# Attention outputs of two heads: sixteen 32-column matmuls, or eight of 64 columns with a copy per head

## What is computed

```python
# HEADS = 16, DIM_HEAD = 64, WINDOW = 32; per batch and head, w = 32 queries per window
bk2, bv2 = (look(bk), look(bv))        # the keys and values of the previous and the own window: 64
sim = jnp.einsum('bhwie,bhwje->bhwij', bq, bk2) * QK_SCALE
sim = jnp.where(mask, -jnp.finfo(sim.dtype).max, sim)
attn = jax.nn.softmax(sim, -1)
out = jnp.einsum('bhwij,bhwje->bhwie', attn, bv2)      # <- the product that is changed
```

## Time and profile before

| | us |
|---|---|
| three runs | 2413.82, 2416.41, 2401.31 (median 2413.82) |
| the profiled execution, its time | 2405.99 |
| the profiled execution, its span | 2404.1 |
| TensorE matmul busy | 2066.7 (86%) |
| VectorE busy | 1774.6 (74%) |
| ScalarE busy | 1492.8 (62%) |
| TensorE weight loads busy | 1431.0 (60%) |

### The profile page before, as it was taken

One profiled execution on the slowest core, in us unless ns is written; L12 is line 12 of the kernel. 1 busy time (PEld: TensorE's weight loads), 2 busy tenths in 40 slices (PEclk: granted clock), 3 DMA queues, 4 the chain that ended last, 5 costly groups with the idle time before them and its releaser, 6 DMA issues. The chain is left out here.

```text
span 2404.1 us, 81162 instructions
## 1 busy us (share of the span) xinstructions
PE 2066.7 (86%) x33532; PEld 1431.0 (60%) x33532; DVE 1774.6 (74%) x3984; ACT 1492.8 (62%) x5170; POOL 1256.0 (52%) x869
## 2 busy tenths in 40 slices
PE   5549999899999999989999999999999964763377
PEld 2337767576675766747667576675766732432255
DVE  4669779597795977959779597795977836685754
ACT  2239769497785976849769497684876823451122
POOL 1138668386783857838678386783865701221000
PEclk8679999999999999999999999999999985885699
DMA  2011111111111111111111111111110100001000
GB/s 96 0 36 41 30 31 54 38 44 30 33 53 37 46 28 35 51 37 44 30 35 53 35 44 30 34 51 38 40 30 25 42 1 12 1 0 54 1 0 17
DMA packets 86557, 80.34 MB, mean 33 GB/s; under 512 B 15040, under 2 KB 82624, under 8 KB 85568
## 3 DMA queue, kind: packets, MB, share of 16 engines
q1 hardware_dynamic: 86208, 75.37, 10.9%
HBM read 25.51 MB, written 1.05 MB: 11 GB/s over the span
## 5 line engine op out<-in xcount | busy, mean ns | idle before, releaser
L984 POOL TENSOR_TENSOR RN<-N,minus_half 128x8 f32<-128x8 f32 x384 | 632.6, 1648 | 158.1 <-DVE N L916 157.1
L822 ACT ACTIVATE PB<-PS,NMX 128x64 f32<-128x64 f32 x1536 | 461.9, 312 | 126.2 <-DVE NMX L950 126.0
L663 PE MATMUL PS<-WQ,XS 128*128 128x256 f32 x1536 | 398.7, 383 | 13.9 <-SPq L538 13.0
L822 ACT ACTIVATION_READ_ACCUMULATOR PB<-PS,NMX 128x1 f32 x1536 | 311.1, 203 | 0.0
L979 POOL TENSOR_TENSOR RR<-R1B,R 128x512 f32<-128x512 f32 x192 | 244.4, 1273 | 103.8 <-DVE QK L940 103.8
L979 POOL TENSOR_TENSOR RR<-R 128x512 f32<-128x512 f32 x192 | 245.4, 1278 | 97.7 <-DVE QK L940 97.7
L663 PEld LDWEIGHTS PS<-WQ,XS 128*128 128x128 f32 x1536 | 264.1, 192 | 35.3 <-SPq L538 13.3
L916 DVE TENSOR_REDUCE N<-SQ 128x8 f32<-128x512 f32 x384 | 259.4, 675 | 5.5 <-ACT SQ L810 5.4
L933 DVE TENSOR_TENSOR R<-PS,SINL 128x512 f32<-128x512 f32 x384 | 262.0, 682 | 1.0 <-POOL RR L979 1.0
L940 DVE SCALAR_TENSOR_TENSOR QK<-RN,RR 128x512 f32<-128x512 f32 x384 | 261.2, 680 | 0.0
L650 PE MATMUL PS<-ident,QK 128*128 128x128 f32 x1536 | 252.1, 287 | 1.8 <-DVE QK L940 1.8
(11 more groups left out here) (210 smaller groups left out, 3582.9 us busy)
## 6 DMA issues: line engine op xcount, KB each, us to landing
VS<-XB SPq DMA_DIRECT2D x384, 96.0 KB
VS<-XB SPq DMA_DIRECT2D x288, 32.0 KB
WQ<-in_wqkv SPq DMA_DIRECT2D x40, 192.0 KB, 2.4
WO<-in_wo SPq DMA_DIRECT2D x6, 512.0 KB, 3.7
BIG<-in_wgu SPq DMA_DIRECT2D x1, 2048.0 KB, 8.7
W<-in_w SPq DMA_DIRECT2D x6, 341.0 KB, 4.0
WQ<-in_wqkv SPq DMA_DIRECT2D x1, 1536.0 KB, 12.0
QKS<-in_qks SPq DMA_DIRECT2D x6, 256.0 KB, 3.4
```

The costliest lines, as they stand in the source:

```text
L663: mm = nc.tensor.matmul(PQ[:, (g + 3) % 2, j * 256:(j + 1) * 256], XSb[b][:, t0:t0 + P], WQ[:, pair * 384:pair * 384 + 256], start=True, s ...
L822: ex = nc.scalar.activation(PB[:, g % 2, u, :], SC[:, h, DH * t:DH * t + DH], ACT.Exp, bias=NMX[:, u:u + 1], accum_out=PSUMS[:, g % 2, u:u ...
L984: nc.gpsimd.tensor_tensor(RN[:, g % 2, :], N2[:, g % 2, :], minus_half[:, :], ALU.pow)
```

## The change

L682 becomes eight matmuls. Each has as stationary operand the values of both heads (64 keys x 128 features), and as moving operand the probabilities of both heads for one window (two runs of 32 columns, 128 apart). Its output is 128 partitions x 64 columns, of which two quarters are wanted: head 0's rows with head 0's queries, head 1's rows with head 1's. The other two (one head's values with the other's probabilities) are computed and not read. `PO` is used to column 256 of each bank in place of 128. The copy to `OTS` becomes two copies of 64 partitions, one per head, and the second one gives `o_free`.

```diff
@@ TensorE, attention outputs
                             for w in range(4):
                                 for t in range(2):
-                                    for h in range(2):
-                                        keys = slice(2 * WIN * t, 2 * WIN * t + 2 * WIN)
-                                        vals = VX if w % 2 else VS
-                                        cols = 256 + P * h + WIN * w
-                                        mm = nc.tensor.matmul(
-                                            PO[DH * h:DH * h + DH, t, WIN * w:WIN * w + WIN],
-                                            vals[keys, c, w // 2, DH * h:DH * h + DH],
-                                            XB[keys, g % CH, cols:cols + WIN],
-                                            start=True, stop=True)
+                                    keys = slice(2 * WIN * t, 2 * WIN * t + 2 * WIN)
+                                    vals = VX if w % 2 else VS
+                                    probs_of_heads = XB[keys, g % CH, 256:512].rearrange(
+                                        "p (h w q) -> p w h q", h=2, w=4)[:, w, :, :]
+                                    mm = nc.tensor.matmul(
+                                        PO[:, t, 2 * WIN * w:2 * WIN * w + 2 * WIN]
+                                        .rearrange("p (h q) -> p h q", h=2),
+                                        vals[keys, c, w // 2, :], probs_of_heads,
+                                        start=True, stop=True)
                             mm.then_inc(o_ps.sem, 1)
@@ ScalarE, copy of the attention outputs
-                            nc.scalar.activation(
-                                OTS[:, pair, c * CB * P:(c + 1) * CB * P]
-                                .rearrange("p (j t q) -> p t j q", j=CB, t=2),
-                                PO[:, :, 0:P].rearrange("p t (j q) -> p t j q", j=CB), ACT.Copy)\
-                                .then_inc(o_free.sem, 1)
+                            for h in range(2):
+                                rows = slice(DH * h, DH * h + DH)
+                                o = nc.scalar.activation(
+                                    OTS[rows, pair, c * CB * P:(c + 1) * CB * P]
+                                    .rearrange("p (j t v q) -> p t j v q", j=CB, t=2, v=2),
+                                    PO[rows, :, 0:256].rearrange("p t (j v n q) -> p t j v n q",
+                                                                 j=CB, v=2, n=2)[:, :, :, :, h, :], ACT.Copy)
+                            o.then_inc(o_free.sem, 1)
```

## The result

| | before | after |
|---|---|---|
| runs, median | 2412.14 us (2401.31 to 2416.41, 4 runs) | 2520.63 us (2518.75 to 2521.61, 4 runs) |
| ratio, 95% interval | | 1.0466 (1.0441 to 1.0490) |
| profiled execution, span | 2404.1 us | 2519.5 us |

2520 us was forecast, in a range of 2480 to 2556. The change costs 108 us by the medians and 112 by the ratio.

A forecast was written before the change was run, and what follows sets the result against it. The bound was taken to be a loop in which VectorE's L926 releases L703. L682's +0.45 us less 0.13 of room, over 342 steps, plus 1 us gave +110 us: 2520 us forecast, range 2480 to 2556.

The forecast's parts named there:

- What bounds the kernel: Attention step of 3.46 us: VectorE's L926 releases TensorE's L703, 0.12 us after its end; L682 is not in the loop.
- The room of 0.13 us: TensorE, beside the wait for L926: L682 may grow by 0.21 - 0.08 = 0.13 us before it holds up L703.
- Passes per tile stay eight, and the load sets a pass: L682 on TensorE: still eight passes; the weight load doubles, a pass goes from 0.057 to 0.113 us, L682 grows 0.45 us.
- The sum: Whole kernel: 342 steps x 0.32 = 109 us, plus 1 for the feed-forward parts: +110 us.
- the waits of L703 for the transfer: L703 waits for the shifted values in 15 steps, 13.0 us; fewer such waits forecast, as the longer period gives the transfer time.
- The copies: ScalarE: two copies holding it 0.26 us each, 0.41 the upper end; cost about 1 us in the feed-forward parts.
- The exponentials: ScalarE: could start at 276.23 but wait for L950 until 276.43, so no cost, with 0.2 us to spare.
- The short load: Rival, 12%: L682's 128-column load stays as short as one of 64, a pass stays 0.057 us; 2417 us.
- The gain from fewer instructions: Rival, 5%: the number of loads and matmuls issued sets L682's length, 0.60 to 0.35 us; 96 us go, 2318 us.
- The missing overlap: Rival, 6%: load and matmul of a tile don't overlap with two tiles, a pass is 0.17 us; about 2680 us.

The follow-up runs named there:

- E5: Kernel before with half of L682's matmuls: two of four windows, each with 64 moving columns in one run; 2412.21 us, ratio 1.0026.
- E6: Kernel before with the four matmuls of L682's last window written twice, two more passes (0.117 us); 2419.66 us, ratio 1.0040.
- E7: Kernel before with the matmuls of L682's last window written three times, four more passes (0.234 us); 2458.17 us, ratio 1.0206.
- E3: Changed kernel with one copy and only head 0's 32 moving columns per matmul, weights still 128 columns; 2498.63 us, ratio 1.0376 against the kernel before.
- E4: Kernel before, sixteen matmuls with weights of 64 columns, but each with 64 moving columns of both heads, and one copy; 2406.71 us, ratio 0.9996.
- E1: Changed kernel with one copy of all 128 partitions in place of two of 64; 2510.01 us, ratio 1.0423 against the kernel before.
- E2: Kernel before with the copy of the outputs split into two of 64 partitions, matmuls untouched; 2422.86 us, ratio 1.0070.
- V2: Kernel before with TensorE's value projection (L711) moved ahead of the transposes of the probabilities (L703); 2379.40 us, ratio 0.9882.
- E8: Kernel before with the copy of the outputs made twice over all 128 partitions, the first into a spare tensor; 2414.36 us, ratio 1.0016.
- V1: Kernel before with VectorE's normalising (L926) moved ahead of the first rotary product (L922); 2407.34 us, ratio 1.0003.

## Why the prediction was right

- **What bounds the kernel.** L926, not L682, released L703, though TensorE was busy for all of the step. E5 shows it: half of L682's passes bought nothing.
- **The room of 0.13 us.** E6 fits in, E7 exceeds it by 0.10. Shown from both sides.
- **Passes per tile stay eight, and the load sets a pass.** 0.112 us a pass measured, 0.113 forecast; E3 and E4 part load and matmul. L682 grew by 0.44 us, 0.45 forecast.
- **The sum: right by two errors that cancel.** The typical step grew by 0.305 us (on average 3.462 to 3.767), 0.32 forecast. Over the first 380 steps of the profiled executions, the steps without a feed-forward part grew by 99 us together, 109 forecast, and the eleven with one by 11 us, 1 forecast. So 110 is met, and 2520 to a microsecond, in part by luck. The 99 are what 326 steps of 0.305 would make and not 342: the steps right behind the feed-forward parts didn't grow (4.26, 4.25 us), and the waits of L703 for the transfer, 13.0 us, are gone, as was forecast. (The rows add the waits of loads and of matmuls, so the 15 steps of the earlier trace rows are fewer: 9 in the loads' own count.)
- **The copies: a term mis-sized.** I took 0.26 us for each, which is what the whole copy holds; the half copies hold 0.39, near the upper end of 0.41. What was forecast as 1 us for the feed-forward parts came out as 10 (E1 against the change): 4 from the later start of these parts, 5 with falls of the clock.
- **The exponentials: not delayed, with nothing to spare where 0.2 us was forecast.** Two errors meet here too. With 0.39 for each copy, the forecast's own working puts the exponentials at 276.49, 0.06 behind the 276.43 at which L950 lets them go; its "0.05 with 0.41 for a copy" holds for one of the two copies only. They came in time because the copies started 0.30 us late and not 0.45, as L803 had waited for L797 and not for L682.
- **The rivals.** The short load fell by the 188 ns. The gain from fewer instructions fell by the eight passes, each of which took longer, and by E5. The missing overlap fell by passes of 0.112, not 0.17.

What stays open: whether the copies bring about the falls of the clock in the feed-forward parts, and what makes the slower executions of E2 slower.

## What to carry to other kernels

Before matmuls on separate tiles of the array are merged, count the passes per tile and ask what fills one: here merging two column tiles left the passes per tile as they were and doubled the columns of each weight load; before, two loads of half the width ran on the two tiles side by side. An engine that is busy for all of a step need not be its bound; look for a start that keeps a fixed distance from another engine's end, and measure the room beside it. Where such a wait is found, independent work of the same queue, moved ahead of it, takes what the room is worth (V2: 29 us). And a sum that comes out right is to be checked term by term.

## What the runs showed of the hardware

- A ScalarE copy of 256 elements from PSUM over 64 partitions held the engine for 0.39 us when it stood beside another half or in front of a whole operation; the same copy over 128 partitions held it for 0.26 to 0.28, overlapped with the next (the kernel before, E1, E8; the halves: the change, E2). Half the partitions cost more, not less. That it is the change of partitions between neighbours that forbids the overlap is my guess; no run parts it from the count of partitions.
- The same VectorE operation (L926) took 0.67 us in the median where a GpSimd addition of two SBUF tensors ran beside its first part, and 0.41 us in its old place (V1); no run parts the addition from the place.
- In the feed-forward parts the granted clock fell from 1.00 to 0.50 for some 3 us in some steps and not in others of the same kernel, 1.7 us each. In the step shown under E1, TensorE had been at 1.00, idle for 0.87 us and then busy for 0.5 us, when it fell; the same place in E1 kept 1.00 after the same idle time.
- Float32 weight loads are recorded with 106 ns for 32 columns and 136 for 64 (64 rows), and with 188, 191 and 192 for 128 (64, 85 and 128 rows); those of the transposes by an identity take 141 for 128. Four tiles side by side took a load each every 0.057 us at 64 columns, two tiles every 0.112 at 128.
